# A graph network's Sage passes: the target one-hots of two cells written by one comparison of pairs

## The reference

```python
def _sage_conv(h, src, dst, W_l, b_l, W_r, num_nodes):
    msgs = h[src]
    agg = jax.ops.segment_sum(msgs, dst, num_segments=num_nodes)
    deg = jax.ops.segment_sum(jnp.ones((src.shape[0],), h.dtype), dst, num_segments=num_nodes)
    mean = agg / jnp.maximum(deg, 1.0)[:, None]
    return mean @ W_l + b_l + h @ W_r
h = jax.nn.relu(_sage_conv(x, src, dst, W1_l, b1_l, W1_r, n))
out = jax.nn.relu(_sage_conv(h, src, dst, W2_l, b2_l, W2_r, n))
```

## Time and profile before

| | |
|---|---|
| median of 3 runs | 10362.1 us (10341.73 to 10376.41) |
| span of the profiled execution | 9217.4 us |
| its own time outside the span | not given; the median lies 1144.7 us above the span |
| mean granted TensorE clock | 0.801 |
| Sage passes | from about 4958 to 6870 us of the span, with `sage1`'s closing work and the next pass's preparation between 5800 and 5960 |

### The profile page before, as it was taken

The page is one execution under the profiler, slowest core; times in us unless marked ns, Lnnn a source line. Parts: engine busy times, 40 slices in busy tenths (PEclk is TensorE's granted clock), DMA queues, the critical chain, the costliest instruction groups (busy, mean ns, idle before and its releaser), DMA issues. The chain is left out here.

```text
span 9217.4 us, 249498 instructions
## 1 busy us (share of the span) xinstructions
PE 7101.9 (77%) x84292; PEld 6261.9 (68%) x84292; DVE 6545.3 (71%) x18880; ACT 3179.6 (34%) x6051; POOL 4540.8 (49%) x3929
## 2 busy tenths in 40 slices
PE   6577566666666999999977999799975666666666
PEld 6344566666666888898876888688864555555555
DVE  3899444444435999999986888488864777777775
ACT  1000111111123666666654666366631111111111
POOL 1788777777710000000003666166633777777774
PEclk9676788888857999999997999699975665555665
DMA  5412333333303323322322334133422222222221
GB/s 62 58 42 43 95 100 103 100 101 102 100 21 93 93 93 92 93 93 93 92 70 80 102 102 102 54 101 102 103 61 38 51 49 51 50 50 51 51 51 41
DMA packets 718460, 697.33 MB, mean 76 GB/s; under 512 B 394630, under 2 KB 523494, under 8 KB 717864
## 3 DMA queue, kind: packets, MB, share of 16 engines
q1 hardware_dynamic: 590488, 539.53, 21.5%
q0 software_dynamic: 125776, 150.49, 8.7%
q10 hardware_dynamic: 1728, 0.25, 0.0%
HBM read 639.21 MB, written 50.66 MB: 75 GB/s over the span
## 5 line engine op out<-in xcount | busy, mean ns | idle before, releaser
L805 POOL DMA_INDIRECT soft_G<-soft,soft_idx x1568 | 1599.2, 1020 | 540.7 <-issue 475.6
L805 POOL DMA_INDIRECT msg_G<-msg_src,msg_idx x1176 | 1229.9, 1046 | 364.4 <-issue 353.2
L1765 POOL DMA_INDIRECT sage_chunk_rows<-sage_rows,chunk_src x672 | 1026.5, 1528 | 756.8 <-PE ps L1800 435.4
L669 POOL MEMSET acc<- 96x1280 f32 x30 | 34.4, 1162 | 2570.4 <-POOLq L2192 2260.9
L1809 ACT ACTIVATE sage_G<-ps 128x384 bf16<-128x384 f32 (+1 forms) x2100 | 1018.0, 485 | 682.4 <-PE ps L1820 677.8
L1820 PE MATMUL ps<-T,sage_ohT 128*128 128x192 bf16 x8232 | 1041.8, 248 | 29.4 <-DVE sage_ohT L1732 28.1
L1612 PE MATMUL ps<-att_far,att_ohT 128*128 128x65 bf16 x15582 | 925.9, 194 | 172.0 <-DVE att_ohT L1551 112.4
L1738 DVE TENSOR_SCALAR sage_ohd<-iota,sage_cols 128x256 bf16<-128x256 bf16 x4116 | 917.2, 284 | 198.8 <-PE ps L1832 195.3
L1832 PE MATMUL ps<-sage_G,sage_ohd 128*128 128x192 bf16 x8232 | 1020.1, 245 | 1.9 <-issue 1.9
L1612 PE MATMUL ps<-acc,att_ohT 128*128 128x65 bf16 x15582 | 921.2, 194 | 0.0
L1933 PE MATMUL ps<-ident,soft_G 128*128 128x128 f32 x1568 | 379.4, 422 | 694.1 <-DMA soft_G<-soft,soft_idx 694.1
(11 more groups left out here) (463 smaller groups left out, 14793.0 us busy)
## 6 DMA issues: line engine op xcount, KB each, us to landing
sage_rows<-srow SPq DMA_DIRECT2D x336, 320.0 KB, 3.4
acc<-pair_rows SPq DMA_DIRECT2D x196, 448.0 KB
att_rows<-pair_rows SPq DMA_DIRECT2D x147, 448.0 KB, 3.8
msg_edge<-edge_attr SPq DMA_DIRECT2D x196, 256.0 KB
msg_row<-dst_rows SPq DMA_DIRECT2D x196, 256.0 KB
soft_row<-dst_rows SPq DMA_DIRECT2D x196, 256.0 KB
soft_G<-soft,soft_idx POOLq DMA_INDIRECT x1568
sage_rows<-srow SPq DMA_DIRECT2D x84, 288.0 KB
```

Source lines behind the costliest of these rows:

```text
L669: done(pool.memset(acc[0:TOP, nodes], 0.0), "zeroed")
L805: eng.indirect_dma_start(B["G"][h][:, j, :], None, src_table, bass.IndirectOffsetOnAxis(ap=B["idx"][h][:, j:j + 1], axis=0)).then_inc(gath ...
L1765: pool.indirect_dma_start(chunk_rows[n % 2][:, j, :], None, sage_rows, bass.IndirectOffsetOnAxis(ap=chunk_src[:, n, j:j + 1], axis=0)).the ...
```

## The change

The target one-hots of a step are written by one comparison for both cells, with the two cells as the inner pairs of the tile. `ohd` changes its layout from `[P, 2, SB]` to `[P, SB, 2]`, so the matmuls of line 1832 take every second element as weights. The second operand of a two-tensor comparison is a bf16 tile `colp` in place of the f32 columns; it is cast from `cols` once a group, with a column of zeros behind the 49, and a semaphore `colp` orders this. The first operand is `pair_iota`, each number of `iota256` twice, made once. A group's last step compares both halves too, though it has one cell.

```diff
-                        cols, ohd = buf("cols", [P, NSB]), buf("ohd", [P, 2, SB], BF16, RING)
+                        cols, colp, ohd = buf("cols", [P, NSB]), buf("colp", [P, NSB + 1], BF16), buf("ohd", [P, SB, 2], BF16, RING)
...
                             if q == 0:
                                 dve.wait_ge(cols_in[s // STEPS], (i + 1) * 16)
+                                dve.tensor_copy(colp[s // STEPS][:, 0:NSB], cols[s // STEPS][:])
+                                dve.memset(colp[s // STEPS][:, NSB:NSB + 1], 0.0).then_inc(S["colp"], 1)
                             need(dve, S["summed"], n - RING + 1)
-                            for c in range(m):
-                                ins = dve.tensor_scalar(ohd[s % RING][:, c, :], iota256[:], cols[s // STEPS][:, 2 * q + c:2 * q + c + 1], None, ALU.is_equal)
-                            ins.then_inc(S["ohd"], 1)
+                            dve.wait_ge(S["colp"], g + 1)
+                            both = colp[s // STEPS][:, 2 * q:2 * q + 2].rearrange("p (o t) -> p o t", o=1).broadcast_to([P, SB, 2])
+                            dve.tensor_tensor(ohd[s % RING][:], pair_iota[:], both, ALU.is_equal).then_inc(S["ohd"], 1)
...
                             for c in range(m):
                                 for half in range(2):
-                                    ins = pe.matmul(ps[:, 5 + s // STEPS, half * 3 * D:(half + 1) * 3 * D], ohd[s % RING][:, c, half * P:(half + 1) * P], G[s % RING][:, c, :],
+                                    ins = pe.matmul(ps[:, 5 + s // STEPS, half * 3 * D:(half + 1) * 3 * D], ohd[s % RING][:, half * P:(half + 1) * P, c], G[s % RING][:, c, :],
...
+        pair_iota = chunks_kept.enter_context(nc.sbuf_tensor("pair_iota", [P, SB, 2], BF16))
...
+                dve.tensor_copy(pair_iota[:], iota256[:].rearrange("p (n t) -> p n t", t=1).broadcast_to([P, SB, 2])).then_inc(s_masked, 1)
```

More of the change, by code:

```diff
@@ L1678, in slot_sums @@
             with ExitStack() as scope:
-                S = {n: scope.enter_context(nc.semaphore(f"{name}_{n}")) for n in "ohT ohd gathered taken summed red turned added coff coh csum cadd".split()}
+                S = {n: scope.enter_context(nc.semaphore(f"{name}_{n}")) for n in "ohT ohd gathered taken summed red turned added coff coh csum cadd colp".split()}
                 chunk_in = gathered[0:2]
```

## The result

The changed kernel takes 10563.1 us in the median of four runs (10554.6 to 10566.3), the kernel before 10353.2 (10341.7 to 10376.4): ratio 1.0206, 95% interval 1.019 to 1.0223, so it is slower by 1.9 to 2.2%. The forecast was 10351 and no change.

The account below looks back on a forecast made before the run. PE was taken to bound the Sage passes, with VectorE busy 84% and felt only in a late stretch. Hidden VectorE costs and 0 for strided weights left 11 us of waits saved: 10362.1 - 11 = 10351 us, range 10322 to 10392.

Parts of the forecast that it names:

- The comparison of a step: VectorE, two scalar comparisons replaced by one of two tensors: 390 to 343 ns a step, saving 47 ns.
- The cast: VectorE, first step of a group: copy, memset and a waiting comparison cost 0.46 us, bounds 0.3 and 0.7, hidden by idle time.
- The weights of line 1832: PE, strided stationary operand: 0 us extra taken, bounds 0 to 53 us.
- the two signs that the prediction named for being wrong: Spacing of line 1832's matmuls rising by 5 ns, or the new comparison taking over 390 ns start to start.
- The waits behind VectorE: PE's line 1820 weight loads waiting for `sage_ohT` in the Sage passes: 41.7 us to fall to about 30.
- the 11 us: Forecast gain: 11 of some 12 us of PE's waits for `sage_ohT` outside the pass starts would go.
- the rivals that make it slower: Strided weights cost (0.06, 10404 us at 6 ns), dearer two-tensor step (0.05, 10394 to 10490), comparison at half rate (0.02, 10606).
- the one that makes it faster: PE's matmuls also gain 2 to 4 ns from fewer VectorE reads: 16 to 33 us more, some 10325; chance 0.07.
- the rest: Set-up copy under 0.6 us, SP's queue as before, POOL's chunk fetches waiting for line 1800 alone, other passes untouched.
- the four rivals: Costly strided weights 0.06, PE gaining more than its waits 0.07, dearer two-tensor step 0.05, half-rate comparison 0.02.
- the range: Forecast bounds for the changed kernel's time: 10322 to 10392 us, from the PE-gain rival to part of the strided-weights rival.
- the sum: Span 9217.4 - 11 = 9206.4 us; with the median 1144.7 us above the span, 10362.1 - 11 = 10351 us.

Follow-up runs that it names:

- the second experiment: Kernel before with one edit: line 1832 takes every second element of the unchanged tile as weights, VectorE's work unchanged; ratio 1.001.
- pace three: From the third chunk on, each fetch waits for three more gather steps than the one before: changed kernel 9839.8 us (0.9464), kernel before 9927.7 us (0.9546).
- second profile of the kernel before: Kernel before, no edit, profiled again after the result: 10452.8 us with a span of 10451.0 us.
- first profile of the kernel before: Kernel before, no edit, the profile read ahead of the prediction: span 9217.4 us, against a measured median of 10362.1 us.
- two kernels whose useless work differs in form alone: Changed kernel plus 16 unread comparisons in one run per group: old scalar form 10437.2 us (0.9953), new pair form 10574.2 us (1.0083).

## Why the prediction was wrong

*The comparison of a step* was right. Three take 1.10 us, so 0.34 us start to start (343 forecast), 422 ns each in the mean (425 forecast). *The cast* costs 0.14 us to the memset and 0.16 to the comparison, 0.30 us in place of 0.46, and is hidden:

```profile
5795.05 0.19 DVE L1736 CAST sage_colp<-sage_cols 128x49 bf16<-128x49 f32 x1
5795.19 0.06 DVE L1737 MEMSET sage_colp<- 128x1 bf16 x1
5795.35 1.10 DVE L1741 TENSOR_TENSOR sage_ohd<-pair_iota,sage_colp 128x512 bf16<-128x512 bf16 x3
```

*The weights of line 1832* were right: 0, by the second experiment. Neither of the two signs that the prediction named for being wrong came up: the spacing of those matmuls is 82 ns in the median as before, and the comparison stays under 390 ns.

*The waits behind VectorE* came out as forecast: some 30 us were to be left of the 41.7. With pace three the weight loads of the gather wait 2.7 us for `sage_ohT` and 27.0 us under "issue", where the starts of the passes went in that profile, 29.7 in all; almost without fetches they wait 28.9. In the second profile of the kernel before the two kinds are 41.9 us, in the changed kernel 31.3. So the 11 us are there as waits. A gain of that size in time isn't shown: the Sage part without fetches is 12 us shorter, but the first profile of the kernel before, with all its fetches, is shorter still (1841).

The chances have a slip: the rivals that make it slower add up to 0.13, the one that makes it faster is 0.07, where 0.12 and 0.08 are given.

The step that failed is *the rest*, in its sentence that POOL's chunk fetches wait for line 1800 alone. They are also held up beside VectorE's runs of comparisons, and the page of the kernel before had it: a chunk fetch took 1528 ns in the mean, the same instruction 1020 and 1046 in the edge passes.

```profile
L805 POOL DMA_INDIRECT soft_G<-soft,soft_idx x1568 | 1599.2, 1020 | 540.7 <-issue 475.6
L805 POOL DMA_INDIRECT msg_G<-msg_src,msg_idx x1176 | 1229.9, 1046 | 364.4 <-issue 353.2
L1765 POOL DMA_INDIRECT sage_chunk_rows<-sage_rows,chunk_src x672 | 1026.5, 1528 | 756.8 <-PE ps L1800 435.4
```

I had read POOL as off the critical path and so as free. The change lets the fetches through: 1187 to 973 ns in the mean, and six of the seven distances in a burst of eight are 1.25 us in the median. They then hit what the first profile didn't contain, late signals under dense fetches, and the idle time that these make grows by 127 us (521 to 648). Neither the four rivals nor the range had a way for that.

The second failed sentence is on the sum: "the median lies 1144.7 us above the span, and nothing of the change lies there". Nearly all of the 1144.7 us lay inside the span of the timed executions (2 us lay outside it in the second profile), some 597 of them in the very passes that the change touches. The profile left a ninth of the measured time without an account, and that was a reason to widen the range, and to ask which stages could hold it.

What is shown: the loss comes with the new comparison and not with the weights; without fetches it is gone; pacing the fetches takes it and 5% more away; two kernels whose useless work differs in form alone are 1.3% apart. That the old comparisons were cheaper because they spread the fetches is the reading that fits these, but the last pair shows the form of the work at play and not the spread by itself. What is open: why PE's signals are late under dense fetches and whether the recording has a part in it, why one profiled execution was free of it, and which property of the pair comparisons, as they stand in the change, lets the fetches through where an unbroken run of them doesn't.

## What to carry to other kernels

Before making an engine faster or changing its form, look at whose work it held up: compare the mean duration of the same POOL instruction in stages with and without the neighbour. A burst of indexed fetches that nobody needs for many microseconds can be worth spacing by a wait on a count of steps: two lines of code gave 5.4% here with the change and 4.5% without it, where the forecast of the change was about 0.1%. And when the span of a profile and the measured time don't agree, take that difference as part of the kernel until it is accounted for.

## What the runs showed of the hardware

With indexed fetches of 128 rows 1.25 us apart, PE's signals came 2.0 us late in the median of 329 late ones and 5.2 us at most, from the second fetch of a burst on (some 100 of the 648 us of idle distances lie between the second and the third). ScalarE's signals to PE came on time beside them. With fetches some 2 to 3 us apart PE lost next to nothing by it (98 us of idle distances, 75 of them the gap between passes). One profiled execution of the kernel before had four fetches begun within 5 us in some 130 us of its time, against 490 in the changed kernel, and no late signals, so density alone doesn't make them.

Weights with every second bf16 element load as fast as packed ones: 96 ns at least and 97 in the median, against 95 and 97, at 192 moving columns.

An indexed fetch that takes 0.94 us elsewhere lasted 4.22 us beside an unbroken run of comparisons with a scalar, and 3.42 us beside a run of comparisons of two tensors and a batch of `sage_ohT`.
